# A five-bank ring for the last scores of each batch, and one shared bank for the three small outputs, in a two-stage attention block

## The reference

```python
h = _layernorm(x) * (1 + ca) + sa
x = x + ga * favor_attention(h, Wq, Wk, Wv, Wo, bo, proj)      # 16 heads, 64 features
h = _layernorm(x) * (1 + cb) + sb
for e in range(4):                                             # 512 tokens each
    xm = layernorm(h[:, e*512:(e+1)*512])[..., :256 >> e]
    q, k, v = xm @ q_w[:, :m].T + q_b, ...                     # 8 heads of 32
attn = softmax(q @ k.T / 16) @ v                               # 2048 x 2048 for each head
for e in range(4):
    out_e = attn_e[..., :256 >> e] @ o_w[:m, :m].T + o_b[:m]   # padded to 256 columns
x = x + gb * (concat(out_e) + h)
```

## Time and profile before

| what | value |
|---|---|
| runs | 1776.65, 1781.54, 1785.52 us (median 1781.54) |
| the profiled execution's own time | 1779.44 us |
| its span in the trace | 1777.6 us |
| mean granted TensorE clock | 0.972 of full speed |
| TensorE busy | 1692.4 us (95%) |
| VectorE, GpSimd, ScalarE busy | 1381.0, 1123.3 and 1085.2 us |

### The profile page before, as it was taken

One profiled execution on the slowest core, in us unless ns is written; L12 is line 12 of the kernel. 1 busy time (PEld: TensorE's weight loads), 2 busy tenths in 40 slices (PEclk: granted clock), 3 DMA queues, 4 the chain that ended last, 5 costly groups with the idle time before them and its releaser, 6 DMA issues.

```text
span 1777.6 us, 31990 instructions
## 1 busy us (share of the span) xinstructions
PE 1692.4 (95%) x11538; PEld 972.0 (55%) x11538; DVE 1381.0 (78%) x2629; ACT 1085.2 (61%) x2066; POOL 1123.3 (63%) x1058
## 2 busy tenths in 40 slices
PE   6999989999999989999999998999999999899998
PEld 4775544444577554444467755444437765444443
DVE  5987977776588788787678878877848878778783
ACT  1885536666688543666668844466667875356664
POOL 2784358677678344876767734686776862477774
PEclk8999989999999999999999999999999999899999
DMA  5000360010200045001110005400120001620201
GB/s 187 2 1 2 111 178 15 19 46 24 73 1 2 1 151 143 10 19 46 57 40 2 1 14 176 105 19 10 46 72 25 2 1 51 187 64 12 50 5 48
DMA packets 56077, 89.57 MB, mean 50 GB/s; under 512 B 13288, under 2 KB 31976, under 8 KB 53100
## 3 DMA queue, kind: packets, MB, share of 16 engines
q1 hardware_dynamic: 54768, 87.45, 17.0%
q10 hardware_dynamic: 1152, 0.07, 0.0%
HBM read 49.29 MB, written 35.72 MB: 48 GB/s over the span
## 4 chain that ended last, share of the span: by engine, by line
PE 69%; DVE 16%; ACT 8%; DMA 2%; issue 2%; SPq 2%; POOL 1%; ACTq 0%; DVEq 0%; POOLq 0%
PE PS L1695 14%; PE PS L1522 13%; PE PS L1707 12%; PE PS L1720 7%; PE PS L1416 5%; DVE MXP L1103 4%; PE PS L1441 3%; PE PS L1424 3%; PE PS L1451 3%; ACT HT L662 2%; ACT HTR L665 2%; DVE STAT L996 2%; DVE QKS L1171 1%; ACT PHIQ L703 1%; PE PS L1571 1%
## 5 line engine op out<-in xcount | busy, mean ns | idle before, releaser
L623 POOL TENSOR_TENSOR TS<-PR 128x1024 f32<-128x1024 f32 (+1 forms) x248 | 551.3, 2236 | 273.6 <-ACT PR L893 208.8
L1103 DVE TENSOR_REDUCE MXP<-PS 128x1 f32<-128x512 f32 x960 | 588.8, 681 | 145.2 <-PE PS L1522 144.6
L893 ACT ACTIVATE PR<-PS 128x512 f32<-128x512 f32 x960 | 487.5, 624 | 302.0 <-PE PS L1695 282.4
L1522 PE MATMUL PS<-KOP,QOP 96*128 96x512 f32 x960 | 406.2, 436 | 9.6 <-DVE MXP L1103 3.3
L1695 PE MATMUL PS<-QOP,KOP 97*128 97x512 f32 x960 | 389.7, 429 | 8.8 <-ACT PR L893 5.7
L1522 PEld LDWEIGHTS PS<-KOP,QOP 96*128 96x128 f32 x960 | 186.2, 195 | 168.9 <-issue 89.6
L1695 PEld LDWEIGHTS PS<-QOP,KOP 97*128 97x128 f32 x960 | 179.9, 189 | 153.1 <-ACT PR L893 130.1
L1707 PE MATMUL PS<-PR,V 128*32 128x512 f32 x1920 | 256.1, 607 | 0.0
L1707 PEld LDWEIGHTS PS<-PR,V 128*32 128x32 f32 x1920 | 65.8, 113 | 150.2 <-issue 110.8
L1720 PE MATMUL PS<-TS,ones 128*32 128x512 f32 x960 | 139.2, 618 | 0.0
L541 POOL TENSOR_SCALAR PK<-XSK 128x1024 f32<-128x1024 f32 x64 | 67.1, 1048 | 102.2 <-ACT XSK L725 102.2
(11 more groups left out here) (157 smaller groups left out, 2559.4 us busy)
## 6 DMA issues: line engine op xcount, KB each, us to landing
KOP<-k_scr SPq DMA_DIRECT2D x84, 256.0 KB, 5.6
k_scr<-QKS SPq DMA_DIRECT2D x64, 256.0 KB, 2.9
QOP<-q_scr SPq DMA_DIRECT2D x180, 64.0 KB, 2.0
q_scr<-QKS SPq DMA_DIRECT2D x40, 256.0 KB, 2.9
X<-in_L_attn_x_dram SPq DMA_DIRECT2D x16, 512.0 KB, 3.9
out_dram<-X SPq DMA_DIRECT2D x12, 512.0 KB, 2.9
QOP<-MXT SPq DMA_DIRECT2D x224, 0.5 KB
KOP<-QKS SPq DMA_DIRECT2D x36, 64.0 KB, 2.0
```

Of the source, the lines that this page charges most:

```text
L623: g.tensor_tensor(sums(k)[:, 0:len(stage)], pair[:, :, 0], pair[:, :, 1], ALU.add).then_inc(S["psum_t"], 1)
L893: a.activation(PR[:, k % 2, w, q], bank(score_bank(p, n, w, q)), ACT.Exp).then_inc(S["ex"], 1)
L1103: v.tensor_reduce(MXP[:, u % 2, i, kc:kc + 1], bank(max_bank(p)), AX.X, ALU.max).then_inc(S["am_rd"], 1)
L1522: mm(bank(max_bank(p)), QOP[0:96, u % QS6, i * P:(i + 1) * P], KOP[0:96, h % KS6, kc * CH:(kc + 1) * CH], start=True, stop=True).then_inc( ...
```

## The change

Three things change, all in the softmax attention.

1. From slot 54 on (`WIDE_SLOT`, the first slot of pair 27; `WIDE` is its score number, 200) scores go round the banks 0, 1, 5, 3, 4 (`WIDE_RING`), and a score waits for the exponential five before it instead of three. Every score of slot 54 also waits until VectorE has read all maxima blocks (`am_rd`), since these used the banks 0 and 1.
2. The three small outputs go to bank 2, and each is issued between `values(2m)` and `values(2m + 1)` instead of after both.
3. The first transpose of the next batch element, which also uses bank 2, waits until VectorE has read the three small outputs (`fin`).

```diff
@@ def out_ps(e):
-            if e == 0:
-                return bank(2, 2)
-            return bank(0) if e == 1 else bank(1)[:, (0 if e == 2 else 4 * width[2]):][:, 0:TPC * width[e]]
+            return bank(2)[:, 0:TPC * width[e]]
...
@@ def score_bank(p, n, w, q):
-            return 3 + (exps(0, p, n, w, q) - 1) % 3
+            i = exps(0, p, n, w, q) - 1
+            return WIDE_RING[(i - WIDE) % 5] if i >= WIDE else 3 + i % 3
+
+        def score_free(b, p, n, w, q):
+
+            i = exps(0, p, n, w, q) - 1
+            return exps(b, p, n, w, q) - (5 if i >= WIDE else 3)
+
+        WIDE_SLOT = 2 * ((NU * MAXU - LOOK) // 8)
+        WIDE = exps(0, WIDE_SLOT // STEPS, WIDE_SLOT % STEPS, 0, 0) - 1
+        WIDE_RING = (0, 1) + tuple(3 + (WIDE - 3 + i) % 3 for i in range(3))
...
@@ def score(k, w, q):
+                    if k == WIDE_SLOT:
+                        pe.wait_ge(S["am_rd"], NU * MAXU * (b + 1))
                     if k > 1 or exps(0, p, n, w, q) > 3:
-                        pe.wait_ge(S["ex"], exps(b, p, n, w, q) - 3)
+                        pe.wait_ge(S["ex"], score_free(b, p, n, w, q))
...
@@ the loop over pairs
                     if 2 * m == SLOTS - 2 and following is not None:
+                        pe.wait_ge(S["fin"], (NC + 1) * b + NC - 1)
                         x_transposes(following, 0, 0, 0)
                     denominators(m - 1)
                     values(2 * m)
-                    values(2 * m + 1)
                     for i, e in enumerate(results[:-1]):
                         if 2 * m == OUT_SLOTS[e]:
                             output(i)
+                    values(2 * m + 1)
```

## The result

The changed kernel takes 1765.69 us (median of 4, 1765.24 to 1768.27) against 1780.88 for the kernel before on the same footing; the ratio is 0.9924 with a 95% interval of 0.9909 to 0.9939 (the two medians alone divide to 0.9915, inside it). It is faster by 0.8%, more than the 0.5% that can be told from no change, and 5.7 us above the forecast of 1760. Run again beside other kernels it took 1767.94 against 1778.21, a ratio of 0.9939 (0.9926 to 0.9951), so the gain is 10 to 15 us, where 21.5 were forecast.

A forecast was written before the change was run, and what follows sets the result against it. TensorE bounds the kernel, its last five pairs per batch element paced by ScalarE's exponentials through three banks. 1779.4 less 13.0 (3.26 us times four) and 8.5 for the clock gives 1757.9, with the runs' median 2.1 above: 1760, range 1754 to 1774.

The forecast's parts named there:

- rival (a): Pairs 27 to 31: the ring works but the clock still falls there or next to them, 1768.5 us; chance 0.2.
- The wider ring: Last five pairs: five scores go out at once, three are paced; denominators start 0.98 us earlier, at T + 2.67.
- The moved output: Pairs 27 and 29: the output's 1.0 us fills a 0.2 us wait for the last exponential; both save the whole 0.98.
- Pair 28: ScalarE's stage-end copy and first exponential end up in a row, losing 0.34 of the 0.98 us: 0.64 saved.
- Pair 30: No output here; last values start at about 4.70, it ends at T + 5.62 and saves 0.71 us at full clock.
- the 3.31 in the sum: Pairs 27 to 30, full clock, per batch element: savings of 0.98, 0.64, 0.98 and 0.71 us.
- Pair 31, a loss of 0.05 us: GpSimd's sum ends at T + 6.64, denominators begin at 6.7; VectorE's sum of slot 63 ends no later, at T + 6.2.
- rival (b): Pairs 27 to 29: another engine, GpSimd the candidate, becomes the bound and the gain misses the end, 1777.5 us; chance 0.11.
- The new waits: Waits for last maxima, second result and third output read: all put at nothing, with 1.4 and 2.0 us of cover.
- The granted clock: Five half-clock falls in pairs 27 and 30, 1.70 us each, all vanish: 8.5 us, a guess within 0 to 8.5.
- rival (c): Slower: denser bank switching makes the clock fall in all 20 pairs, 15 more falls of 1.70 us, 1794; chance 0.05.

## Why the prediction was right, and where it was off

The direction and the mechanism of the ring held, and the time lies in the range of 1754 to 1774. The size is another matter: the two profiled executions differ by 11.1 us and the medians by 10 to 15, where 21.5 were forecast. The 1765.7 lies nearer to the 1768.5 of rival (a), for which the range had been drawn so wide, than to the forecast, though (a)'s condition, falls of the clock in these pairs, did not come true. That the range holds is in part luck: it was open to a miss by the clock, and a miss in pair 31 filled the room. Point by point, by the steps of the prediction:

- *The wider ring, 0.98 us a pair.* The denominators start at T + 2.68, forecast 2.67, and the ring of four gives half. Shown.
- *The moved output.* It was to fill a wait of 0.2 us. The ring without the move shows a wait of 0.3 us in pair 27 (value sums of 2.21 us instead of 1.90), and the move gains 0.17 of it. What the move cuts in two costs the rest: from denominators to next score the changed pair 27 takes 3.85 us (1293.06 to 1296.91) where 3.72 was assumed. Pair 27 takes 6.53 us instead of 6.39 and pair 29 6.62 instead of 6.31; in the latter the output takes 1.09 us (1308.28 to 1309.37 in the timeline) instead of 0.91 when value sums follow it rather than scores.
- *Pair 28* was to lose 0.34 us to ScalarE's copy. With the first output alone put back behind the value sums it takes 6.48 us instead of 6.84, so the copy costs 0.36. Shown. That the pair takes 6.84 and not the 6.68 of the sum comes from the cut value sums again.
- *Pair 30*: 5.69 instead of 5.62.
- So the pairs 27 to 30 save 2.63 us at the full clock (28.31 to 25.68) instead of the 3.31 in the sum, 10.5 instead of 13.2 over four batch elements.
- *Pair 31, a loss of 0.05 us*: this is the step that failed: the sum of slot 63 was put at its old length. GpSimd's sum of slot 62 ended 6.55 us into the pair, where the prediction had 6.64, but VectorE's was put at T + 6.2, its 1.54 us simply added, and it ended at T + 7.63. The two sums overlap in time now, and before they had hardly done so. The last output starts 1.0 us later in the pair than before in two batch elements, and 2.5 in the first, where a stretch at half clock follows the idle time, 4.5 us in all where the sum had 0.2. In its kind this is rival (b), another engine that becomes the bound, though in pair 31 and not in the pairs 27 to 29, whose denominators wait for no sum.
- *The new waits* cost nothing: no wait for maxima or `fin` shows in these pairs.
- *The granted clock, 8.5 us.* All five falls in the pairs are gone. Over all ten profiles, counting the pairs 27 to 30: with a ring of three there were five falls in sixteen pairs in each of three kernels; with four none in sixteen; with five one in 96, over six profiles. So a ring of three brings falls here and a wider one hardly any, and rival (c), a fall in every pair, did not come. That it is the paced stretch that does it, and not something else that changes with the ring, is argued and not shown; nor is what picks the pairs.
- *New falls* came elsewhere: one right behind pair 31 in the first batch element (463.3 to 466.7, granted 0.53) and one at the very end, where the last output takes 3.35 us instead of 1.99. TensorE had been idle 2.03 us before the first and 1.44 before the last. Neither idle time brings a fall by itself: the 2 us stand in the next two batch elements and in the second profile of the same kernel without one, and the 1.44 in the kernel before. On TensorE, from the changed kernel's timeline:

```profile
462.25 1.14 PE L1730 MATMUL PS<-TS,ones 128*32 128x512 f32 x8 [2.03 <-DVE TS L1289]
463.32 2.93 PE L1424 MATMUL PS<-W1T,HTR 128*128 128x512 f32 x6
...
1759.68 3.35 PE L1787 MATMUL PS<-OWG,NUM 128*128 128x256 f32 x8 [1.44 <-DVE NUM L1328]
```

The saving in the two profiles adds up thus: the stretch from pair 27 to pair 31 is 19.0 us shorter over four batch elements (121.7 to 102.7), 4.5 go in pair 31, 1.4 in the last output, and 2.0 were lost in the stretches between one batch element's last output and the next one's pairs, nearly all between the third and the fourth, in parts that the change doesn't touch. That loss comes again in the second profile and in that of the ring alone; its cause stays open. That leaves 11.1, the difference of the spans (1777.6 to 1766.5). In the medians it is 10 to 15.

The Trainium skill ("SBUF — State Buffer", "SBUF: two separate sides") says that VectorE, in an operation with two SBUF inputs, and GpSimd, in one that reads SBUF, share a pair of memory ports as an exclusive lock, and that the one that comes second waits for the whole instruction of the other. The trace agrees: VectorE's sum ends 1.08 us behind GpSimd's, not 1.23 behind its own start. That is 0.15 us less than its whole length of 1.23, so the wait is for nearly all of it. In the kernel before, the rows had already shown it: the sum of slot 63 started at 1332.01 beside GpSimd's (1330.10 to 1332.47) and ended at 1333.55, again 1.08 us behind it. Had the prediction read its own rows by that rule, the sum would have been put at 6.64 + 1.08 = 7.72 us into pair 31, against 7.63 measured.

## What to carry to other kernels

Where a ring of buffers paces the producer, each further buffer is worth one consumer's step in each round (0.49 us here), until the work behind the ring waits for the last consumer; then it is that wait that decides, and something useful must stand in it. When a part gets shorter, list the instructions of VectorE and GpSimd that it pushes into the same time: two that never met before may now take turns, and it can pay to move one of them to the other engine. Here that brought another 8 to 10 us, of which the profiles show 5.4 to be the earlier sum. A stretch in which TensorE is paced by another engine can cost more than its idle time: here five falls of the clock stood behind such stretches, and they went with them.

## What the runs showed of the hardware

- VectorE's sum of two SBUF halves (128x1024) took 1.23 us alone, 1.54 when it met the last 0.45 us of GpSimd's sum of the same size, and 2.96 when it met 1.9 us of it; each time it ended 1.08 to 1.09 us behind that sum. GpSimd's own sum took 2.36 to 2.38 in all cases, but its small instructions behind a VectorE sum were stretched: 0.73 to 1.71, 1.23 to 2.04 and 0.57 to 1.55 us.
- A stretch at half clock lasted 3.4 us each time in these pairs, and cost 1.6 to 1.7 us in the kernels with a ring of three, whichever pair it hit, and 1.3 in the one such pair with a ring of five (7.96 against 6.64).
